# Lower parts of four weight tiles subtracted by GpSimd, and the splits of the output weights spread one by one

## The reference, cut to what matters

```
x = layernorm(x + attention(x))                 # x: 4 batches x 512 rows x 512
x = layernorm(x + scan_block(ctx, gate=x))      # state-space scan, 16 states x 512 channels
x = layernorm(x + experts(x))                   # shared expert + 16 routed ones, top 8

attention: qkv = h @ Wqkv.T + b                 # 16 query, 8 key, 8 value heads of 128
  p = softmax(q1 k1) - lam * softmax(q2 k2)     # causal, two maps subtracted
  o = rmsnorm(p @ v) * subln * (1 - LAMBDA_INIT);  return o @ out_w.T + out_b
scan_block, for each step t:
  state = state * exp(dt*A) + (dt*u) * B[t];  y[t] = sum_n state[n] * C[t][n]
```

## Time and profile before

| | us |
|---|---|
| median of three runs | 1616.1 |
| the profiled execution's own time | 1615.29 |
| its span | 1613.4 |
| busy in the span: PE / DVE / POOL / ACT | 1397.1 / 1294.5 / 1137.9 / 1045.1 |
| mean granted TensorE clock | 0.933 of full speed |

### The profile page before, as it was taken

One profiled execution on the slowest core, in us unless ns is written; L12 is line 12 of the kernel. 1 busy time (PEld: TensorE's weight loads), 2 busy tenths in 40 slices (PEclk: granted clock), 3 DMA queues, 4 the chain that ended last, 5 costly groups with the idle time before them and its releaser, 6 DMA issues.

```text
span 1613.4 us, 23141 instructions
## 1 busy us (share of the span) xinstructions
PE 1397.1 (87%) x7536; PEld 1139.5 (71%) x7536; DVE 1294.5 (80%) x2377; ACT 1045.1 (65%) x2411; POOL 1137.9 (71%) x613
## 2 busy tenths in 40 slices
PE   3655789999999989899989899986579998998996
PEld 1213678877888978788878788874367676776784
DVE  4898688998888998888989899898548577486575
ACT  3888466766666767667657666664458567577474
POOL 1335489888889987789988799998576266266263
PEclk8777889999999999999999999998799999999998
DMA  5485636667856675765666765675342122112121
GB/s 166 151 292 205 187 93 172 172 153 170 215 150 138 173 178 155 210 150 126 177 189 168 188 161 123 159 188 107 113 143 79 27 94 77 59 60 65 31 68 60
DMA packets 130313, 225.50 MB, mean 140 GB/s; under 512 B 11704, under 2 KB 61376, under 8 KB 128656
## 3 DMA queue, kind: packets, MB, share of 16 engines
q1 hardware_dynamic: 120400, 188.36, 36.9%
q0 software_dynamic: 9792, 35.66, 14.2%
HBM read 145.99 MB, written 77.99 MB: 139 GB/s over the span
## 4 chain that ended last, share of the span: by engine, by line
PE 40%; DVE 23%; issue 12%; POOL 11%; ACT 8%; DMA 5%; SPq 1%; POOLq 0%; DVEq 0%; ACTq 0%
PE banks L607 10%; PE banks L609 9%; PE banks L608 9%; POOL act_buf L1976 5%; DVE negmax L1118 3%; PE banks L1522 3%; DMA x_lo<-scratch_xs 3%; PE banks L1523 2%; PE banks L1524 2%; DVE state L1178 2%; DVE prob L1132 2%; DVE banks L423 1%; DVE banks L2051 1%; DVE qT_lo L1108 1%; ACT banks L944 1%
## 5 line engine op out<-in xcount | busy, mean ns | idle before, releaser
L1311 POOL TENSOR_TENSOR state<-state,Cn 128x1024 f32<-128x1024 f32 x100 | 244.9, 2449 | 74.9 <-DVE state L1178 74.0
L1976 POOL TENSOR_TENSOR act_buf<-act_buf,wb 128x512 f32<-128x512 f32 x128 | 165.5, 1294 | 172.3 <-ACT act_buf L1882 170.2
L1286 POOL TENSOR_TENSOR state<-dtu_sb,Bn 128x1024 f32<-128x1024 f32 x103 | 249.1, 2419 | 27.3 <-DMA Bn<-scratch_bc 25.5
L1178 DVE TENSOR_TENSOR_SCAN state<-banks,state 128x512 f32<-128x512 f32 x206 | 249.8, 1213 | 2.6 <-ACT banks L998 1.8
L998 ACT ACTIVATE banks<-dt_sb,negA 128x512 f32<-128x512 f32 x256 | 177.1, 692 | 91.0 <-DVE state L1178 72.7
L607 PE MATMUL banks<-x_hi,w_hi 128*128 128x512 f32 (+1 forms) x512 | 190.1, 371 | 47.1 <-DVE qT_lo L1108 13.3
L609 PE MATMUL banks<-x_hi,w_lo 128*128 128x512 f32 (+1 forms) x512 | 180.8, 353 | 0.0
L608 PE MATMUL banks<-x_lo,w_hi 128*128 128x512 f32 (+1 forms) x512 | 180.3, 352 | 0.0
L607 PEld LDWEIGHTS banks<-x_hi,w_hi 128*128 128x128 f32 x512 | 103.0, 201 | 68.6 <-issue 27.8
L2051 DVE TENSOR_TENSOR banks<-banks,act_buf 128x512 f32<-128x512 f32 x136 | 94.3, 694 | 49.9 <-POOL act_buf L1976 26.1
L2041 DVE TENSOR_TENSOR hid_lo<-banks,hid_hi 128x512 fp32r<-128x512 f32 x136 | 93.7, 689 | 46.2 <-ACT hid_hi L1894 44.3
(11 more groups left out here) (226 smaller groups left out, 4592.8 us busy)
## 6 DMA issues: line engine op xcount, KB each, us to landing
scratch_y<-state POOLq DMA_DIRECT2D x52, 512.0 KB, 5.9
x_hi<-scratch_xs SPq DMA_DIRECT2D x32, 512.0 KB, 5.8
x_lo<-scratch_xs SPq DMA_DIRECT2D x32, 512.0 KB, 9.2
Cn<-scratch_bc SPq DMA_DIRECT2D x64, 256.0 KB, 3.8
Bn<-scratch_bc SPq DMA_DIRECT2D x64, 256.0 KB, 4.1
scratch_acc<-acc_sb SPq DMA_DIRECT2D x64, 256.0 KB, 2.1
wb<-scratch_wT SPq DMA_DIRECT2D x64, 256.0 KB, 3.3
acc_sb<-scratch_acc SPq DMA_DIRECT2D x48, 256.0 KB, 3.1
```

The source lines that it names most:

```text
L1178: nc.vector.tensor_tensor_scan(row, dA[:, :], row, 0.0, ALU.mult, ALU.add) \
L1286: nc.gpsimd.tensor_tensor(ring(k), dtu[:, 2 * h:2 * h + 2, :], Bn[:, state % NB, :].unsqueeze(1).broadcast_to([P, 2, T]), ALU.mult).then_i ...
L1311: nc.gpsimd.tensor_tensor(to, ring(k), Cn[:, state % NB, :].unsqueeze(1).broadcast_to([P, 2, T]), ALU.mult).then_inc(S["gated"], 1)
L1976: nc.gpsimd.tensor_tensor(act_[:, N % 3, :], act_[:, N % 3, :], wb[:, E % 3, :], ALU.mult) \
```

## The change

Two things are changed. First, the low parts of the keys' and values' stages (c = 0, 1, 6, 7) of the groups 1 to 3 are computed by POOL, at loop turn k = the index in `W_AT`, behind `drive(k+3)` and ahead of the DMA of an odd turn. These four are not scaled, so a plain subtract does. POOL waits for the low parts before it and for the high part. DVE, which still does the other stages, waits at c = 2 and c = 8 until POOL's two low parts ahead of it are done. Second, the output weights' stages are no longer split two and two: on both engines stage 9 comes behind the projection at the end of the same step, stage 11 behind the squares on ACT and behind scan 4p+1 and `row_max(2p+1)` on DVE.

```
+PLAIN = (0, 1, 6, 7)
@@ ACT, step p
             if p % 16 == 2 and p < NM:
                 stage_high(NSTAGE * (p // 16) + 10)
-                stage_high(NSTAGE * (p // 16) + 11)
             if 1 <= p <= NM:
                 squares(p - 1)
+            if p % 16 == 2 and p < NM:
+                stage_high(NSTAGE * (p // 16) + 11)
             if p < NM:
                 decay(4 * p + 2)
                 softmax(2 * p + 1)
...
             if p % 16 == 1 and p < NM:
                 stage_high(NSTAGE * (p // 16) + 8)
-                stage_high(NSTAGE * (p // 16) + 9)
             if 2 * p + 1 + AHEAD < NPROJ:
                 proj_high(2 * p + 1 + AHEAD)
             if 2 * p + 1 in W_AT:
                 stage_high(W_AT[2 * p + 1])
+            if p % 16 == 1 and p < NM:
+                stage_high(NSTAGE * (p // 16) + 9)
@@ DVE, stage_low(n)
             dve.wait_ge(S["stage_hi"], n + 1)
+            if n >= 8 and c in (2, 8):
+                dve.wait_ge(S["stage_lo"], n)
@@ DVE, step p
-            if 2 * p in W_AT:
+            if 2 * p in W_AT and W_AT[2 * p] % NSTAGE not in PLAIN:
                 stage_low(W_AT[2 * p])
...
             if p % 16 == 2 and p < NM:
                 stage_low(NSTAGE * (p // 16) + 10)
-                stage_low(NSTAGE * (p // 16) + 11)
             if p < NM:
                 scan(4 * p + 1)
                 row_max(2 * p + 1)
+            if p % 16 == 2 and p < NM:
+                stage_low(NSTAGE * (p // 16) + 11)
...
             if p % 16 == 1 and p < NM:
                 stage_low(NSTAGE * (p // 16) + 8)
-                stage_low(NSTAGE * (p // 16) + 9)
             if p < NM:
                 scan(4 * p + 3)
             if 2 * p + 1 + AHEAD < NPROJ:
                 proj_low(2 * p + 1 + AHEAD)
-            if 2 * p + 1 in W_AT:
+            if 2 * p + 1 in W_AT and W_AT[2 * p + 1] % NSTAGE not in PLAIN:
                 stage_low(W_AT[2 * p + 1])
+            if p % 16 == 1 and p < NM:
+                stage_low(NSTAGE * (p // 16) + 9)
@@ POOL
+        def stage_low(n):
+            c = n % NSTAGE
+            pool.wait_ge(S["stage_lo"], n)
+            pool.wait_ge(S["stage_hi"], n + 1)
+            cut = slice(TILE_COL[c], TILE_COL[c] + HD)
+            nc.gpsimd.tensor_tensor(w[1][:, :, cut], stage[:, n % 2, :].rearrange("p (k n) -> p k n", k=KT),
+                                    f32(w[0][:, :, cut]), ALU.subtract).then_inc(S["stage_lo"], 1)
@@ POOL, turn k
             if k + 3 < NDRIVE:
                 drive(k + 3)
+            if k in W_AT and W_AT[k] % NSTAGE in PLAIN:
+                stage_low(W_AT[k])
```

## The result

The changed kernel takes 1657.07 us (median of 4 runs, 1655.81 to 1659.02), the kernel before 1615.61 us beside it on the same chip: 1.0263 times as long, 95% interval 1.0235 to 1.0291, 41.5 us slower. The forecast was slower, 1637 us, with a range from 1616 to 1649: the sign was right, the size half of what came, and the measured time lies 8 us above the range.

What follows compares the result with a forecast made beforehand. No single engine was taken as the bound: PE and DVE take turns, so queue waits decide. Terms 10.8 + 14.0 + 0 - 1.5 + 0 + 5 = 28.3, less 6.3, gave +22.0 on 1615.3: 1637 us, range 1616 to 1649.

Steps and rivals of the forecast that it cites:

- Stage 2: DVE waits for POOL's stage 1, then for POOL's next product; PE stands still 3.6 us a group, 10.8 us in all.
- Stage 11: DVE's low part misses its turn against POOL's product, so PE's output product starts 3.5 us later; four groups, 14.0 us.
- Stage 9: Behind the projection, PE gains at most 2.6 us, but it meets POOL's product; taken as 0, bounds -2.6 and +2.
- Stages 6 and 7: DVE is rid of 5.7 us in all, a quarter of it on the path: -1.5 us, bounds -5.7 and 0.
- SP's and POOL's queues: Loads wait for POOL, drive(24) is some 4 us late, unseen by DVE and PE: 0, upper bound 12 us.
- Rival (d): POOL becomes the bound; late B rows and added subtracts make drives late for their scans, 1649 us; chance 5%.
- Clock: Seven new PE gaps of 3.5 and 3.6 us, likely followed by a lower clock: +5 us, bounds 0 and 16.
- The part given back: ACT and POOL work on during the two stalls; a quarter of 24.8 us returns in the following step, 6.3 us.

Runs made afterwards that it cites:

- experiment 2: Kernel before, with only stages 0 and 1 on POOL and DVE's wait at stage 2, output weights unchanged: 1625.15 us, 1.0066 against the kernel before.
- experiment 3: Kernel before, with only stages 6 and 7 on POOL and DVE's wait at stage 8: 1628.79 us, 1.0085 against the kernel before.
- experiment 5: Only stages 6 and 7 on POOL, with SP's even-index stage loads issued behind the load of B's row: 1620.62 us, 1.0032 against the kernel before.
- experiment 1: Changed kernel with all low parts back on DVE, only the output weights' stages split one by one: 1634.03 us, 1.0125 against the kernel before.

## Why the prediction was right in its direction and short in its size

- **Stage 2:** predicted +3.6 us a group, 10.8; measured +3.9 to +4.1, 11.9. The mechanism is the forecast one to its parts: idle 2.38 us for POOL, then a lost race and 2.77 us. The gain ahead of it is seen for one step, 1.0 us at step 10, and is lost in the wait, as forecast.
- **Stage 11:** predicted +3.5 us, 14.0; measured 16.3 in the changed kernel, 15.4 alone. The clock fell behind the gap of 3.75 us, and the forecast counts the clock in a term of its own; that this is the whole difference is not shown.
- **Stage 9:** predicted 0, and it meets POOL as foretold (2.43 us in step 17); +3.1 us measured beside it, the upper bound was +2. Of these, 0.4 a group is in groups 0 and 3; of the 1.3 at step 18, some 0.9 stands in experiments 2 and 3 also, which leave stage 9 alone. So what is stage 9's own is rather 0.4 us a group, within the bound.
- **Stages 6 and 7:** predicted -1.5; alone they bring -2.8 us at steps 13, 29 and 45 (experiment 3), of which 1.6 are the shorter fall of the clock in group 2. That leaves -1.2, near the forecast.
- **SP's and POOL's queues, the step that failed.** I wrote that POOL would find its B row some 4 us late and that "DVE and PE don't see it: 0". The first half is right: POOL waits 4.10 us for B's row in front of drive(24) (at 349.36) and 3.80 us in step 13. The second counted only those who wait for POOL's *results*, three turns ahead. It left out that POOL and SP also issue the large DMAs of the batch change, which now run beside the store that SP waits for and beside the load of x, and PE waits for x without any reserve (1.88 us of idle time before the change). That cost 18.5 us, the largest single item. Experiments 3 and 5 show that the price comes from the late B row in SP's queue: +14.4 us, +5.6 with SP's order changed. Rival (d) had POOL's lateness cost something, with the scans as its victims; it was the load of x. That the DMAs falling together is what delays x is read from the traces (the loads of dtu and dt beside the store of output rows, the store of y beside the loads of x, PE's gap 5.52 against 2.20 us); no run moved one of these alone, so it is the likely link and not a shown one.
- **Clock:** +5 over seven gaps, on the ground that gaps of this length are followed by a fall. It fell behind stage 11, but behind stage 2 in none of the three groups (1.00 over 7 us from 345, 594 and 845 us), although those gaps are 2.86, 2.84 and 2.84 us; it fell some 12 us later, behind gaps of only 2.0 to 2.2 us. In experiment 2 the same stall, 2.97, 2.86 and 2.89 us, was followed by a fall at once (0.76, 0.53 and 0.53). The length of a gap alone does not tell whether a fall follows. Beside the forecast places it fell at step 17, 3 us a group.
- **The part given back, -6.3** (a quarter of 24.8 is 6.2; the working also ends at 1637.3 for the profiled execution and 1638.1 for the median, not 1637): -7.4 us came at the steps 13 to 15, but not as I wrote it. ACT's and POOL's work during the waits gives nothing back: behind a stall the difference of the two traces stands within 0.05 us for six steps. About 6.8 of the 7.4 us are the clock, whose fall moved from behind the wait for x to before it, where that wait covers it. No forecast of mine had this.

With step 17's 18.5 us in the place of the queue's 0 the sum of +22.0 would have been +40.5, against 41.2 measured between the traces. That the other errors cancel to 1 us is luck: the stages 2, 11 and 9 cost 6.5 us more than forecast, 5 us of clock were counted apart, and the gain at the steps 13 to 15 came from something else than the forecast gain.

## What to carry to other kernels

A piece of work moved to another engine brings its position in that engine's queue with it: look at what stands before it, what stands behind it (that will run at the moment when the waiting engine wakes), and at every queue that waits for its buffer. When an engine becomes late, ask not only who waits for its results but which large transfers it issues, and what they will then meet. Order on the same engine matters at a few tenths of a microsecond where two engines exclude each other: put the short operation ahead of what releases the other engine, not behind. And when two traces are compared, look at the granted clock before a difference of 1 to 2 us is put down to an edit.

## What the runs showed of the hardware that I had not expected

- Subtracts of two SBUF operands on DVE and tensor operations of POOL exclude each other fully, and 0.14 to 0.17 us decide: 0.17 us ahead 0.73 us (POOL 2.81), 0.14 behind 2.74 us (POOL 2.33). It strikes a subtract of one row as well (1x512: 0.73 us, or 2.95). DVE, woken by POOL's signal, lost to POOL's next operation each time at stage 2 (three of three in the changed kernel, DVE 0.15 to 0.17 us behind).
- The length of one gap of PE does not decide what the granted clock does. Over 7 us it was 1.00 behind a gap of 2.84 us in the changed kernel (594 to 601 us), 0.53 behind one of 2.86 us in experiment 2 (581 to 588 us), and 0.76 behind one of 2.24 us in the changed kernel (358 to 365 us). After one of 3.75 us it was 0.72 over 6 us and then 0.50; after one of 5.35 us 0.50 for 6 us.
- The same gap in a place that no edit touched was followed by a longer or shorter low stretch from one kernel to the next (0.76, 0.51, 0.76 in the kernel before, 0.58, 0.76, 0.53 in experiment 1), worth 1.3 to 1.7 us a group either way.
